# Four graph layers on one core: two of each 16 edge columns by one-hot products in bf16 instead of one in fp32

## The reference, cut to what matters

```python
# layer 0 (4 heads x 32)              # layer 1                         # layer 3
msg = alpha[:, :, None] * xh[row]     msg = edge_weight[:, None]*x[src]  ex = jnp.exp(e - m[dst])
out = segment_sum(msg, col)           agg = segment_sum(msg, dst)        # weighted sum of h[src] over dst
```

## Time and profile before

| | us |
|---|---|
| median of 3 runs | 6681.86 (6681.67 to 6683.09) |
| profiled execution: span from first to last instruction | 6678.7 |
| VectorE busy | 5046.5 (76%) |
| GpSimd busy | 4583.7 (69%) |
| TensorE busy (matmul) | 3332.5 (50%) |
| first to last fetch issued in the passes of layers 0, 1, 3 | 920.4, 918.8, 917.7 |

### The profile page before, as it was taken

One profiled execution on the slowest core, in us unless ns is written; L12 is line 12 of the kernel. 1 busy time (PEld: TensorE's weight loads), 2 busy tenths in 40 slices (PEclk: granted clock), 3 DMA queues, 4 the chain that ended last, 5 costly groups with the idle time before them and its releaser, 6 DMA issues. The chain is left out here.

```text
span 6678.7 us, 61345 instructions
## 1 busy us (share of the span) xinstructions
PE 3332.5 (50%) x21638; PEld 2959.0 (44%) x21638; DVE 5046.5 (76%) x7174; ACT 1003.4 (15%) x2297; POOL 4583.7 (69%) x4753
## 2 busy tenths in 40 slices
PE   7530117467777457777468857730000004777770
PEld 5530106357777457777443327730000003777770
DVE  8999998778898677787647779986343446888886
ACT  1013333200000010000034435520000003000002
POOL 0027777677777677777667777777777767777774
PEclk9999558788989778888779988865555556888885
DMA  3036011134444344444339974433343332333332
GB/s 60 1 148 256 2 32 18 26 85 115 115 112 113 101 115 110 110 110 110 99 124 345 343 283 122 126 88 107 103 108 104 103 92 59 112 112 112 112 112 71
DMA packets 588107, 763.09 MB, mean 114 GB/s; under 512 B 118267, under 2 KB 479585, under 8 KB 568345
## 3 DMA queue, kind: packets, MB, share of 16 engines
q1 hardware_dynamic: 416916, 375.57, 17.7%
q0 software_dynamic: 152672, 272.57, 17.1%
q10 hardware_dynamic: 18210, 111.02, 4.2%
HBM read 346.63 MB, written 412.16 MB: 114 GB/s over the span
## 5 line engine op out<-in xcount | busy, mean ns | idle before, releaser
L1103 POOL DMA_INDIRECT l2z_rows<-proj,l2z_idx x784 | 764.5, 975 | 246.2 <-issue 238.6
L2685 POOL DMA_INDIRECT l2s_krow<-table_k,l2s_idx x762 | 721.8, 947 | 232.2 <-issue 230.4
L1103 POOL DMA_INDIRECT l0z_rows<-table,l0z_idx x736 | 697.3, 947 | 234.7 <-issue 224.0
L927 POOL DMA_INDIRECT l3z_rows<-table,l3z_idx x736 | 694.6, 944 | 234.7 <-issue 224.0
L1103 POOL DMA_INDIRECT l1z_rows<-table,l1z_idx x736 | 694.6, 944 | 233.5 <-issue 213.0
L836 PE MATMUL l3z_pfound<-l3h_hn,l3h_hot 128*128 128x130 f32 x4800 | 645.1, 303 | 233.9 <-DVE l3h_hot L813 233.9
L836 PE MATMUL l1z_pfound<-g_x,l2o_xT 128*128 128x128 f32 x4800 | 638.3, 303 | 238.9 <-DVE l2o_xT L813 238.9
L836 PEld LDWEIGHTS l3z_pfound<-l3h_hn,l3h_hot 128*128 128x128 f32 x4800 | 637.2, 218 | 241.8 <-issue 234.7
L836 PEld LDWEIGHTS l1z_pfound<-g_x,l2o_xT 128*128 128x128 f32 x4800 | 630.5, 218 | 246.6 <-issue 239.0
L2097 POOL DMA_INDIRECT first_sj<-scores,first_atdst x504 | 504.7, 1001 | 170.7 <-issue 170.7
L836 PE MATMUL l0z_pfound<-first_rows,l0r_hot 128*128 128x140 f32 x3648 | 468.0, 292 | 82.0 <-DVE l0r_hot L813 81.9
(11 more groups left out here) (619 smaller groups left out, 7639.4 us busy)
## 6 DMA issues: line engine op xcount, KB each, us to landing
proj<-l2s_proj ACTq DMA_DIRECT2D x100, 1024.0 KB
spread_q<-prep_zero SPq DMA_DIRECT2D x98, 656.0 KB
l2s_zrow<-spread_q SPq DMA_DIRECT2D x98, 656.0 KB, 4.8
prefix<-l0z_acc SPq DMA_DIRECT2D x196, 256.0 KB, 3.1
prefix<-l2o_kn SPq DMA_DIRECT2D x196, 256.0 KB
prefix<-l2z_acc SPq DMA_DIRECT2D x196, 256.0 KB
prefix<-l3z_acc SPq DMA_DIRECT2D x48, 1040.0 KB, 4.1
l2z_rows<-proj,l2z_idx POOLq DMA_INDIRECT x784, 2.6
```

Of the source, the lines that this page charges most:

```text
L927: nc.gpsimd.indirect_dma_start(out=rows[:, k % RING, u, :], out_offset=None, in_=table, in_offset=bass.IndirectOffsetOnAxis(ap=idx[:, lo + ...
L1103: nc.gpsimd.indirect_dma_start(out=rows[:, k % RING, c * (hi - lo) + u, :], out_offset=None, in_=table, in_offset=bass.IndirectOffsetOnAxi ...
L2685: nc.gpsimd.indirect_dma_start(out=krow[:, k % KRING, c * (hi - lo) + u, :], out_offset=None, in_=g.table_k, in_offset=bass.IndirectOffset ...
```

## The change

Two columns of each 16 are picked (one of each last 8), so 98 columns a pass and not 48; 686 and not 736 are fetched. The one-hot matrix is bf16. The node table is split in three bf16 pieces: the high one is the upper half of the fp32 word itself, read with a step of 2; middle and low are made by VectorE (`Pieces`), three instructions for each group of blocks, in the tails before layers 1 and 3 and at the start of the pass of layer 0. Each block then takes two products: 256 columns (middle, low) and 128 (high); 280 + 140 in layer 0, 260 + 130 in layer 3. VectorE adds the two sums (`move`) into `rows`, in place of ScalarE's copy. ScalarE takes the partition's base off the turned numbers and writes them as bf16 to SBUF (`dig`). The marks are spread over the batch (`share`) and made two batches ahead (`AHEAD`). `RING` is 4. PSUM is laid out anew, with the last 8 columns of `keep` read from SBUF. In layers 1 and 3 the marks of a pick are two instructions of 25 blocks, in layer 0 four of 12 or 13 blocks.

```diff
-WIDTH, RING, ACCS = 16, 6, 2
+WIDTH, RING, ACCS, PICKED = 16, 4, 2, 2
...
+class Pieces:
...
+    def make(self, chain, b):
+        v, x, rest, ml = self.nc.vector, self.nodes[:, b], self.rest[:, 0:b.stop - b.start], self.ml[:, b]
+        chain(v.tensor_tensor(rest, x, x.bitcast(BF16)[:, :, 1::2], ALU.subtract))
+        chain(v.tensor_copy(ml[:, :, 0], rest.bitcast(BF16)[:, :, 1::2]))
+        chain(v.tensor_tensor(ml[:, :, 1], rest, ml[:, :, 0], ALU.subtract))
...
+AHEAD = 2
+BANK = 512
+SHARES = 5
...
 class Picks:
...
-        self.base, self.names = s.sb("pbase", [P, 1]), s.sb("pnames", [P, NB])
-        self.code, self.found = s.ps("pcode", [P, P]), s.ps("pfound", [P, nodes.shape[2]])
+        self.base, self.blocks = s.sb("pbase", [P, 1]), s.sb("pblocks", [P, NB, 16], BF16)
+        self.digit = s.sb("pdigit", [P, 2, P], BF16)
+        self.code = s.ps("pcode", [P, BANK])[:, 0:P]
+        self.found = [s.ps(f"pfound{h}", [P, BANK])[:, 0:2 * self.width].rearrange("p (t f) -> p t f", t=2) for h in range(2)]
...
-            self.nc.vector.tensor_tensor(self.hot[i][:, 0:hi - lo], bc_mid(self.code[:], hi - lo), bc_last(self.names[:, lo:hi], P),
-                                         ALU.is_equal).then_inc(self.hotted, 1)
...
+    def mark(self, eng, at):
+        n, i = at // self.parts, at % self.parts
+        lo, hi = self.cuts[i], self.cuts[i + 1]
+        if i == 0:
+            eng.wait_ge(self.dug, n + 1)
+        if at >= len(self.hot):
+            eng.wait_ge(self.summed, at - len(self.hot) + 1)
+        out = self.hot[at % len(self.hot)].rearrange("p b (r q) -> p b r q", q=16)
+        names = self.blocks[:, lo:hi].unsqueeze(2).to_broadcast([P, hi - lo, P // 16, 16])
+        digit = self.digit[:, n % 2].rearrange("p (r q) -> p r q", q=16).unsqueeze(1).to_broadcast([P, hi - lo, P // 16, 16])
+        self.nc.vector.tensor_tensor(out, names, digit, ALU.is_equal).then_inc(self.hotted, 1)
+
+    def move(self, eng, rows, k):
+        n = self.moved
+        found = self.found[n % 2]
+        eng.wait_ge(self.summed, self.parts * (n + 1))
+        self.nc.vector.tensor_reduce(rows[:, k % RING, self.slots[n]], found.rearrange("p t f -> p f t"), AX, ALU.add).then_inc(self.placed, 1)
+        self.moved += 1
...
+    def on_vector(self, eng, rows, k, share):
+        todo = self.of(k + AHEAD)
+        lo, m = todo.start * self.parts, len(todo) * self.parts
+        for at in range(lo + m * share // SHARES, lo + m * (share + 1) // SHARES):
+            self.mark(eng, at)
+            if at % self.parts == self.parts - 1 and at // self.parts >= 2:
+                self.move(eng, rows, self.batch_of(self.moved))
...
+        t, high = self.nc.tensor, self.nodes.bitcast(BF16)
+        for n in self.of(k + AHEAD):
...
+            if n + 2 < self.count:
+                pe.wait_ge(self.dug, n + 2)
+                self.name(n + 2)
+            if n >= 2:
+                pe.wait_ge(self.placed, n - 1)
...
+                for b in range(self.cuts[i], self.cuts[i + 1]):
+                    hot = self.hot[at % len(self.hot)][:, b - self.cuts[i]]
+                    t.matmul(found.rearrange("p t f -> p (t f)"), hot, self.ml[:, b].rearrange("p t f -> p (t f)"), start=b == 0, stop=False)
+                    mm = t.matmul(found[:, 0], hot, high[:, b, 1::2], start=False, stop=b == NB - 1)
...
+    def dig(self, act, n):
...
+        self.nc.scalar.activation(self.digit[:, n % 2], self.code, ACT.Identity, bias=self.base[:, 0:1]).then_inc(self.dug, 1)
...
                     for u in range(hi - lo):
+                        if picks:
+                            picks.on_vector(eng, rows, k, 1 + u)
...
+CUTS = (0, NB // 2, NB)
...
+    def first(self, chain):
+        for b in range(0, NB, 10):
+            self.pieces.make(chain, slice(b, b + 10))
...
+                    if i >= 2:
+                        eng.wait_ge(normed, GROUPS[i - 2][-1] + 1)
+                        pieces.make(chain, span(GROUPS[i - 2]))
...
+CUTS0 = (0, 12, 25, 37, NB)
```

More of the change, by code:

```diff
@@ L823, in name, with landed @@
+    def landed(self, eng, rows, k):
+        while self.moved < self.first[k + 1]:
+            self.move(eng, rows, k)
+        eng.wait_ge(self.placed, self.first[k + 1])
+    def name(self, n):
+        j = self.columns[n]
+        self.nc.tensor.matmul(self.code, self.g.src[:, j:j + 1].to_broadcast([P, P]), self.g.ident[:],
                               start=True, stop=True).then_inc(self.coded, 1)
     def on_tensor(self, pe, k):
[L826 to L831, removed]
@@ L883, in _ @@
                 picks.start(chain)
-                picks.on_vector(eng, 0)
+                for k in range(-AHEAD, 0):
+                    for share in range(SHARES):
+                        picks.on_vector(eng, rows, k, share)
                 for k, (lo, hi) in enumerate(BATCHES):
@@ L900, in _ @@
                                                ALU.mult, ALU.add).then_inc(summed, 1)
+                    for share in range(1 + (hi - lo) // 4, SHARES):
+                        picks.on_vector(eng, rows, k, share)
                 eng.wait_ge(summed, NC)
@@ L1025, in sum_strands @@
         stored = [s.sem(f"sto{r}") for r in range(ACCS)]
[L1026 to L1028 removed]
+        w = weigh(nc, s, us, es, weighed, rows, msg, room[:, 4 * BANK - NC:])
+        todo = [[((STRANDS - 1) * STRIDE + hi - 1 - i, STRANDS * (hi - lo) - 1 - i) for i in range(STRANDS * (hi - lo) * PICKED // WIDTH)]
+                for lo, hi in TURNS]
+        picks = Picks(nc, s, g, spot, todo, weighed) if spot else None
         def picked(k):
[L1031 removed]
+            return picks.picked(k) if picks else 0
         def landed(k):
@@ L1046, in _ @@
                 chain.add(v.memset(acc[:, ACCS - 1], 0.0))
-                chain(v.tensor_copy(keep[:], by_step(order.keep[:])))
+                chain(v.tensor_copy(keep[:], by_step(order.keep[:])[:, 0:KEPT]))
                 last = by_strand(acc[:, ACCS - 1])[:, :, ABREAST - 1]
+                aside.first(chain)
                 if picks:
                     picks.start(chain)
-                    picks.on_vector(eng, 0)
+                    for k in range(-AHEAD, 0):
+                        for share in range(SHARES):
+                            picks.on_vector(eng, rows, k, share)
                 for k, (lo, hi) in enumerate(TURNS):
@@ L1067, in _ @@
                         here = sums(k)[:, :, u]
-                        chain(v.tensor_tensor(kept[:], last, bc_last(keep[:, lo + u], D), ALU.mult))
+                        going = keep[:, lo + u] if lo + u < KEPT else by_step(order.keep[:])[:, lo + u]
+                        chain(v.tensor_tensor(kept[:], last, bc_last(going, D), ALU.mult))
                         v.tensor_tensor(here, kept[:], by_strand(msg[:, 0:STRANDS * (hi - lo)])[:, :, u], ALU.add).then_inc(summed, 1)
                         last = here
+                    if picks:
+                        for share in range(1 + hi - lo, SHARES):
+                            picks.on_vector(eng, rows, k, share)
                 eng.wait_ge(summed, STRIDE)
@@ L1083, in _ @@
                 if picks:
-                    picks.on_scalar(act, 0, rows[:, 0, WIDTH - 1], weighed)
+                    for k in range(-AHEAD, 0):
+                        picks.before(act, k)
+                        picks.after(act, k)
                 for k, (lo, hi) in enumerate(TURNS):
                     aside.on_scalar(act, k)
+                    if picks:
+                        picks.before(act, k)
                     w.on_scalar(act, k, STRANDS * (hi - lo))
                     if picks:
-                        picks.on_scalar(act, k + 1, rows[:, (k + 1) % RING, WIDTH - 1], weighed)
+                        picks.after(act, k)
             @block.gpsimd
@@ L1100, in _ @@
                             j = c * STRIDE + lo + u
-                            if picked(k) and j == picks.columns[k]:
+                            if c * (hi - lo) + u >= STRANDS * (hi - lo) - picked(k):
                                 continue
@@ L1774, in _ @@
                 done.on_vector(eng)
-                for i in range(n + 2):
+                for i in range(n + 5):
                     if i < n:
```

190 lines of the change are left out of this document (108 added, 82 removed).

## The result

The changed kernel takes 6917.15 us (median of 4 runs, 6916.41 to 6920.85) against 6681.76: ratio 1.0355, 95% interval 1.0342 to 1.0367. That is 235 us slower; the forecast was 363 us slower. The profiled execution has a span of 6914.6 us, 235.9 more than before.

The account below looks back on a forecast made before the run. GpSimd's fetches bound all three passes, before and after. Layers 1, 3 and 0 add 135, 145 and 46 us, the pieces 37: +363 on 6678.7 makes 7042, with 3 around it 7045 us; range 6880 to 7270.

Parts of the forecast that it names:

- layer 0's tail: Stretch behind layer 0's pass: pieces hidden in VectorE's 37.6 us wait for rows, but for last groups and blocked fetches, +10 us.
- What bounds: All three passes: GpSimd never waits and sets the time, 1.25 us a fetch, 18.75 us a batch of 15 before.
- The fetches' saving: Each pass issues 50 fewer fetches, 14 a batch or 17.5 us: alone 62 us a pass, 187 us in all.
- What the marks do to GpSimd: Marks with both inputs in SBUF hold fetches begun meanwhile: 4.0, 4.2, 2.2 us a batch in layers 1, 3, 0.
- Layer 0: Layer 0's pass: half-length marks in pairs cost fetches 2.2 us a batch, period 19.7 us, +46 us.
- VectorE and the moves: Marks 1.82 or about 1 us, moves 0.42 us; VectorE needs 18.5, 16.3, 17.8 us a batch in layers 0, 1, 3.
- TensorE: Products of two picks a batch: 16.5 us with naming, 17.9 in layer 0, hidden under 21.5; far end 21.3 to 24.3.
- the near end: TensorE's low estimate: bf16 at one cycle a column, 0.160 us a block, 16.5 us a batch, 17.9 in layer 0.
- the other estimate: TensorE in layer 0, from the skill's 81 ns: 0.200 us a block, 20.5 us a batch, adding 40 us to that pass.
- Rival 2: Fetches held by marks and TensorE binding too, layer 0 at 22.4 or 24.3 us a batch: 7175 to 7340 us; chance 18%.
- The pieces: Three VectorE instructions, 2.2 us a group: +22 in and behind layer 2's tail, where VectorE sets the pace; together +37 us.
- Rival 1: Bf16 marks do not hold up fetches in the three passes: -89 us, 6593 us, faster than before; chance 13%.

## Why the forecast was right, and where its sizes were off

| stretch | forecast | measured |
|---|---|---|
| layer 1's pass, first to last fetch | 1054 (+135) | 1006.5 (+87.7) |
| layer 3's pass | 1063 (+145) | 1020.9 (+103.2) |
| layer 0's pass | 966 (+46), and +5 of held fetches at the pieces | 959.0 (+38.6, with 9.1 at the pieces) |
| pieces, layer 2's tail and behind | +22 | about +1 |
| layer 0's tail | +10 | +5.6 |
| sum on the span | +363 | +235.9 |

The measured 6917 us lies in the stated range of 6880 to 7270, but 13 us under the narrower 6930 to 7140 that the forecast gave its own mechanism: the losses were at the low end of 3 to 5 us a batch, and the pieces cost some 22 us less than stated.

- **What bounds** held: GpSimd before and after, with 0.30 us of issue and no holds.
- **The fetches' saving** held: 14 steps of 1.249 us a batch, as layer 3 with its digit in PSUM shows (855.2 us).
- **What the marks do to GpSimd** held as a mechanism, and is shown: inputs in SBUF alone bring the loss to the kernel before (+711 us), one input in PSUM alone takes it away (-146 us in layer 1). The rule of the Trainium skill that I cited beside it (SBUF — State Buffer, who interferes with whom: two SBUF inputs contend with a GpSimd instruction that reads SBUF) agrees with both runs. The inference cited with it, that `tensor_tensor` does not starve descriptor generation, does not hold here: all these marks are `tensor_tensor`, and the measurement decides.
- **Its size is the term that was off**: 4.0 us a batch in layer 1, measured 150.9/49 = 3.08; 4.2 in layer 3, measured 3.37. Two slips make the difference. I put the next mark 1.45 us behind the end of the last, one column step, or 1.87 with a move; the timeline has 2895.17 - 2893.91 = 1.26 and 2898.56 - 2896.98 = 1.58, as neighbouring instructions overlap. And I priced a held fetch at the wait from its request to the mark's end, though it then takes 0.82 us where a free one takes 0.94 in all, 0.12 less. With 1.26 and 1.58 the fetch asks at 2.38 and loses 1.26 + 1.81 - 2.38 - 0.12 = 0.57, or 0.89 behind a move: 1.51 and 1.84 less 0.94, what the timeline shows. The first mark of a batch costs 1.0 on average in layer 1. 1.0 + 0.57 + 0.89 + 0.57 = 3.03, against 3.08. So the walk through the phases was the right way; its inputs were 0.1 to 0.3 us off, four times a batch.
- **Layer 0**: 2.2 us a batch, measured 2.11 with the pieces' 9.1 us in it, 1.93 without.
- **VectorE and the moves**: 1.82, 1.02 and 0.42 us, as forecast, and hidden. The 17.8 us a batch forecast for VectorE in layer 3 show once no fetch is held: 17.9.
- **TensorE**: the near end (0.160 us a block) held nearly, with 0.167 in layer 1; in layer 0 a block is 0.181 us (0.118 and 0.063), where the worked near end was 0.175 and the other estimate 0.200. Two picks are 17.2 and 18.7 us where I had 16.5 and 17.9. Rival 2's 21 to 24 us a batch is refuted, but layer 0 was nearer to it than I said: once no fetch is held, TensorE binds the pass.
- **The pieces**: "in layer 2's tail VectorE sets the pace" is the step that failed. The earlier trace rows show the period of VectorE's groups, and I took it for the pace of the tail. The tail ends with GpSimd's 50 scattered stores, one each 1.27 us, and VectorE had been done for 33 us when the last one ended. The 23 us of pieces fit in that.
- **Rival 1** as I worked it out (6593 us) would have been too fast as well: the run with every digit in PSUM is that case, and takes 6622.6. Layer 0's two picks are bound by TensorE and cost more than one: its stretch is 32.8 us longer than before, where the rival had it about even. Layer 1 gains 59.4 us for the rival's 62, layer 3 34.3 (62.5 less the 28.2 behind its last fetch) for 47.

## What to carry to other kernels

Before an operand of a long VectorE instruction is moved from PSUM to SBUF, look at what GpSimd issues beside it: here the place of one operand was worth 146 us in layer 1's pass and 167 in layer 3's, for the 62 us that fewer fetches save in each. Where it happens, look at the maximum of the fetches' durations, not at the median, and lay the two engines' timelines side by side. When a bound is lifted, measure to the next stage's first instruction and not to the last fetch, as an engine that falls behind pays only there. And a tail's pace is read from the engine that ends last in it, not from the period of a busy one.

## What was not expected of the hardware

- An `is_equal` of 3200 bf16 elements takes 1818 ns with one input in PSUM, 1820 with both in SBUF; an fp32 one of 1600 elements with an input in PSUM takes 1822.
- A held fetch finishes 0.81 to 0.83 us after the instruction that holds it, where a free one takes 0.94 from its start; that was so for marks of 1.0, 1.8 and 3.5 us alike.
- At full clock a block of bf16 products of 256 and 128 columns takes 0.167 us in layer 1 (0.108 and 0.058), each with a load of weights whose own record is 98 or 99 ns: the two loads are all but hidden.
